# A software-pipelined Mamba-2 group loop on one core: state matmuls moved ahead of the transposes, out-projection three slots behind its pair

## The reference

```python
h = x * rsqrt(mean(x*x) + EPS) * norm_w             # x: 2 x 256 tokens, 512 wide
proj = einsum('bsd,od->bso', h, in_proj_w)           # gate 8192, hBC 8192 + 2048, dt 128
hBC = silu(causal_conv(hBC, conv_w, conv_b))         # 4 taps
hid, B, C = split(hBC)                               # 128 heads of 64; 8 groups of 128 for B and C
dt = softplus(dt + dt_bias); A_full = -exp(A_log) * dt
hid_dt = hid * dt
M = (C_i . B_j) * exp(segsum(A_full))                # per head, i >= j
y = M @ hid_dt + Dp * hid
yg = y * silu(gate)
yg = yg * rsqrt(mean over the group's 1024 channels of yg**2 + EPS) * gnorm_w
x = residual + yg @ out_proj_w.T
```

## Time and profile before

| | us |
|---|---|
| median of 3 runs (range) | 827.75 (827.05 to 828.55) |
| profiled execution | 823.68 |
| its span | 821.9 |
| TensorE busy | 790.5 (96%), 4319 matmuls |
| VectorE busy | 612.4 (75%) |
| ScalarE busy | 603.8 (73%) |
| GpSimd busy | 615.7 (75%) |
| groups 1 to 6 | 92.1 each, from loop to loop |

### The profile page before, as it was taken

The page is one execution under the profiler, slowest core; times in us unless marked ns, Lnnn a source line. Parts: engine busy times, 40 slices in busy tenths (PEclk is TensorE's granted clock), DMA queues, the critical chain, the costliest instruction groups (busy, mean ns, idle before and its releaser), DMA issues.

```text
span 821.9 us, 13293 instructions
## 1 busy us (share of the span) xinstructions
PE 790.5 (96%) x4319; PEld 610.7 (74%) x4322; DVE 612.4 (75%) x752; ACT 603.8 (73%) x1052; POOL 615.7 (75%) x552
## 2 busy tenths in 40 slices
PE   8799899999999999999999999999999999989897
PEld 7567677777777777777777777777777777767664
DVE  6768987777786867776786867776786867787774
ACT  5778786888688876878688886878688886877442
POOL 6669966799578986799578986799578985795231
PEclk9999999999999999999999999999999999999999
DMA  8433324334234324333233314334233324340001
GB/s 332 148 92 127 129 65 155 128 120 138 90 128 128 128 64 154 128 128 128 90 128 128 128 64 154 128 128 128 90 128 128 128 65 155 128 154 1 4 2 52
DMA packets 48812, 94.93 MB, mean 116 GB/s; under 512 B 3952, under 2 KB 36848, under 8 KB 48784
## 3 DMA queue, kind: packets, MB, share of 16 engines
q1 hardware_dynamic: 48496, 94.06, 34.6%
q10 hardware_dynamic: 288, 0.52, 0.2%
HBM read 93.26 MB, written 1.31 MB: 115 GB/s over the span
## 4 chain that ended last, share of the span: by engine, by line
PE 62%; DVE 17%; ACT 11%; issue 7%; DMA 0%; POOL 0%; ACTq 0%; DVEq 0%
PE ps_z L1093 19%; PE ps_out L1196 15%; PE ps_h L1093 13%; PE ps_y L1183 7%; DVE conv_bc L728 4%; DVE conv L728 4%; ACT decay L531 4%; PE ps_t L1066 2%; ACT L531 2%; ACT conv L477 2%; DVE v L846 2%; DVE yg L852 2%; DVE decay L786 2%; ACT conv_bc L461 1%; DVE y_lo L858 1%
## 5 line engine op out<-in xcount | busy, mean ns | idle before, releaser
L728 DVE SCALAR_TENSOR_TENSOR conv<-ps_h,w_raw,conv 128x510 f32<-128x510 f32 (+2 forms) x192 | 143.2, 746 | 102.1 <-ACT conv L477 97.6
L531 ACT ACTIVATE decay<-csx,cs_own 128x256 f32<-128x256 f32 (+1 forms) x512 | 184.4, 443 | 1.0
L297 POOL TENSOR_TENSOR win_lo<-w_raw,win_hi 128x1024 fp32r<-128x1024 f32 x64 | 153.1, 2392 | 0.9 <-DMA csx<-cs_rows 0.9
L399 POOL TENSOR_TENSOR sqacc<-sqacc,sq 128x512 f32<-128x512 f32 x47 | 69.8, 1486 | 107.1 <-ACT sq L567 107.1
L786 DVE TENSOR_TENSOR decay<-decay,cbm 128x1536 f32<-128x1536 f32 x64 | 126.0, 1969 | 3.6 <-ACT decay L531 3.6
L1183 PE MATMUL ps_y<-decay,hid_dt 128*64 128x256 f32 (+1 forms) x1024 | 98.9, 336 | 16.1 <-DVE hid_dt L835 16.1
L539 ACT ACTIVATE hidT<-conv 128x512 f32<-128x512 f32 x64 | 40.5, 633 | 100.5 <-DVE conv L728 100.5
L1183 PEld LDWEIGHTS ps_y<-decay,hid_dt 128*64 128x64 f32 x1024 | 64.1, 138 | 58.9 <-DVE hid_dt L835 21.8
L337 POOL TENSOR_SCALAR_AFFINE_SELECT csx<-csx 128x512 f32<-128x512 f32 x128 | 102.1, 823 | 0.5 <-DMA csx<-cs_rows 0.5
L1196 PE MATMUL ps_out<-wout_hi,y_lo 128*128 128x512 f32 x252 | 99.9, 396 | 0.0
L1196 PE MATMUL ps_out<-wout_hi,y_hi 128*128 128x512 f32 x252 | 99.5, 395 | 0.0
(11 more groups left out here) (314 smaller groups left out, 1514.2 us busy)
## 6 DMA issues: line engine op xcount, KB each, us to landing
w_raw<-in_wmain SPq DMA_DIRECT2D x64, 772.0 KB, 4.3
csx<-cs_rows SPq DMA_DIRECT2D x128, 256.0 KB, 3.5
bc_raw<-in_wbc SPq DMA_DIRECT2D x8, 517.0 KB, 3.5
ctx_raw<-in_ctx SPq DMA_DIRECT2D x1, 2048.0 KB, 16.2
bc_raw<-in_wffn SPq DMA_DIRECT2D x2, 512.0 KB, 3.8
out_x<-acc SPq DMA_DIRECT2D x4, 256.0 KB, 2.1
acc<-in_x ACTq DMA_DIRECT2D x2, 256.0 KB, 3.9
acc<-in_x SPq DMA_DIRECT2D x2, 256.0 KB, 3.7
```

Of the source, the lines that this page charges most:

```text
L297: eng.tensor_tensor(win_lo[:, r2, :], w_raw[:, r4, 0:W_IN], win_hi[:, r2, :].bitcast(f32), ALU.subtract).then_inc(low_win, 1)
L399: eng.tensor_tensor(sqacc[:], sqacc[:], sq[:, (k - 1) % 2, :], ALU.add).then_inc(pool_sq, 1)
L531: done = eng.activation(decay[:, r2, b, h, lo:lo + n], csx[:, r2, b, h, lo:lo + n], ACT.Exp, bias=cs_own[:, r2, t, h:h + 1])
L728: eng.scalar_tensor_tensor(out=out_b[:, :, back:], in0=src_b[:, :, 0:S - back], scalar=w[:, TAPS - 1 - back:TAPS - back], in1=out_b[:, :, ...
```

## The change

Each part by engine:

- TensorE: a slot is now hidden projection of s, gate projection of s, out-projection of s-3, state matmuls of s-1, transposes of s. At k = 0 and k = 7, where the gate's bank `ps_z` still holds a B or C projection, the out-projection stands ahead of the gate projection. The C.B products move behind the gate projection and use `ps_h` in place of `ps_z`; the channel sums move to k = 2.
- VectorE: `combine` of s-2 comes first, then `hid_dt` of s-1, the group's add (now k = 3), the mask of s-1, the conv of s, `y_lo` of s-2.
- ScalarE: the decays of s come first in slot s (before: the decays of s+1 came last), then the tap, then `y_hi` and `sq` of s-2, the SiLU of B or C, `hidT`, `gate`.
- GpSimd: the sum of squares (of s-3) goes ahead of the splits, the split of the out-weights is that of pair s (before: s+1) and stands behind the selects, `rstd` is raised at the head of k = 3.
- SP: the same transfers. `y_lo` of a pair is now made two slots behind it (before: one), so the wait for it ends one slot later; a wait for `wout_lo` of the same pair is added.

The core of the diff (line numbers of the two files differ by up to 24):

```diff
 
                     if late(s - 3):
                         eng.wait_ge(dve_ylo, s - 3)
+                        eng.wait_ge(low_wout, s - 3)
                     eng.dma_start(w_raw[:, r, :], wmain_d[s]).then_inc(w_in[r], 16)
...
+                if k == 3 and not first:
+                    eng.wait_ge(dve_ms, g)
+                    eng.tensor_tensor(rstd[:], ms[:], half_neg[:], ALU.pow).then_inc(pool_rstd, 1)
                 if not (last and k == PPG - 1):
                     eng.wait_ge(w_in[n4], 16 * (2 * g + (k + 1) // 4 + 1))
-                    if first and 0 < k < 3:
+                    if late(s):
                         eng.wait_ge(pe_gate, s)
-                    if late(s - 2):
-                        eng.wait_ge(pe_out, s - 2)
+                if late(s - 3):
+                    eng.wait_ge(pe_out, s - 3)
...
+                sum_squares(s, g, k, first)
                 if not (last and k == PPG - 1):
                     split_in(n4, (k + 1) % 2)
-                    split_out(n4)
                     eng.wait_ge(csx_in[1 - r2], 32 * (4 * g + (k + 1) // 2 + 1))
                     lower_in(n4, (k + 1) % 2, s + 2)
                     select(1 - r2)
-                    lower_out(n4, s + 2)
+                split_out(r4)
+                lower_out(r4, s + 1)
                 if k == 4:
                     eng.tensor_scalar(wbc_hi[:], bc_raw[:, 0:BC_W], 1.0, 0.0, ALU.mult, ALU.add).then_inc(hi_wbc, 1)
                     lower_bc(g + 2)
 
-                sum_squares(s, g, k, first)
-                if k == 1 and not first:
-                    eng.wait_ge(dve_ms, g)
-                    eng.tensor_tensor(rstd[:], ms[:], half_neg[:], ALU.pow).then_inc(pool_rstd, 1)
...
-                if k == 1 or (first and k == 0):
+                n = (k - 3) % PPG
+                gs = g if k >= 3 else g - 1
+                if n == 0 or (first and k < 3):
                     return
-                eng.wait_ge(act_sq, s)
-                if k == 2:
-                    if late(g):
-                        eng.wait_ge(pe_ss, g)
+                eng.wait_ge(act_sq, s - 2)
+                if n == 1:
+                    if late(gs):
+                        eng.wait_ge(pe_ss, gs)
                     eng.tensor_tensor(sqacc[:], sq[:, 0, :], sq[:, 1, :], ALU.add).then_inc(pool_sq, 1)
                 else:
...
+                if first and k == 1:
+                    tap(s, g, k)
+                    decays(s, k)
+                    scale_context(0)
+                    hidden(s, k)
+                    gates(s, k)
+                    return
+                decays(s, k)
+                if k == PPG - 1 and not last:
+                    tap_bc(0, g + 1, ps_z, conv_bc[:])
                 if k == 0:
                     tap_bc(1, g, ps_z, conv_bc[:])
-                    silu_bc(1, g, conv_bc[:])
-                if k == PPG - 1 and not last:
-                    tap_bc(0, g + 1, ps_z, conv_bc[:])
-                    silu_bc(0, g + 1, conv_bc[:])
-                if not (first and k == 1):
-                    tap(s, g, k)
-                hidden(s, k)
-                gates(s, k)
+                tap(s, g, k)
                 finish_y(s, g, k, first)
-                if not (last and k == PPG - 1):
-                    decays(s + 1, k + 1)
                 if first:
                     scale_context(k - 1)
                 if last and k == 4:
                     scale_context(PPG - 1)
+                if k == PPG - 1 and not last:
+                    silu_bc(0, g + 1, conv_bc[:])
+                if k == 0:
+                    silu_bc(1, g, conv_bc[:])
+                hidden(s, k)
+                gates(s, k)
...
+                if not (first and k < 2):
+                    combine(s, k)
                 if not (first and k == 0):
                     scale_hidden(s, k)
-                if k == 2 and not first:
+                if k == 3 and not first:
                     add_group(g - 1)
+                if not (first and k == 0):
+                    mask(s, g, k)
                 if k == PPG - 1 and not last:
                     conv_group(0, g + 1, ps_z, conv_bc[:])
-                if k == 0:
-                    conv_group(1, g, *((ps_y, gate[:, 1, :]) if first else (ps_z, conv_bc[:])))
-                if first and k == 0:
-                    conv_hidden(s, k)
+                if k == 0 and not first:
+                    conv_group(1, g, ps_z, conv_bc[:])
+                conv_hidden(s, k)
+                if not (first and k < 2):
+                    lower_y(s, k)
+                if k == 0 and first:
+                    conv_group(1, g, ps_y, gate[:, 1, :])
...
                     eng.tensor_copy(cbm[:, 0, :], ps_t[:, 0:MJ]).then_inc(dve_cb, 1)
-                if not (first and k == 0):
-                    conv_hidden(s, k)
-                if k == 1 and not first:
+                if k == 2 and not first:
                     mean_squares(g - 1)
-                if first and k == PPG - 1:
-                    eng.wait_ge(pre_pool, POOL_RSTD + TT)
-                if not (first and k == 0):
...
-                eng.wait_ge(act_exp, s + 1)
-                if k == 0:
-                    eng.wait_ge(dve_cb, 2 * g + 2)
-                eng.tensor_tensor(decay[:, r2], decay[:, r2], cbm[:].unsqueeze(2).broadcast_to([P, B, 2, MJ]),
-                                  ALU.mult).then_inc(dve_m, 1)
-                if not (first and k == 0):
-                    lower_y(s, k)
...
+            def mask(s, g, k):
+
+                eng.wait_ge(act_exp, s)
+                if k == 1:
+                    eng.wait_ge(dve_cb, 2 * g + 2)
+                q2 = (k - 1) % 2
+                eng.tensor_tensor(decay[:, q2], decay[:, q2], cbm[:].unsqueeze(2).broadcast_to([P, B, 2, MJ]),
+                                  ALU.mult).then_inc(dve_m, 1)
...
-                q2, q4 = (k - 1) % 2, (k - 1) % 4
-                eng.wait_ge(pe_y, s)
-                eng.wait_ge(act_hid, s)
-                if late(s - 1):
-                    eng.wait_ge(dve_yg, s - 1)
+                q2, q4 = k % 2, (k - 2) % 4
+                eng.wait_ge(pe_y, s - 1)
+                eng.wait_ge(act_hid, s - 1)
+                if late(s - 2):
+                    eng.wait_ge(dve_yg, s - 2)
...
-                eng.wait_ge(dve_convbc, 3)
-                project(ps_z[:], win_hi[:, 0, KT * P:], win_lo[:, 0, KT * P:], pe_gate)
-
             def slot(eng, s, g, k, first, last):
                 r2 = k % 2
+
+                turned = k == 0 or k == PPG - 1 and not last
 
                 eng.wait_ge(low_win, s + 1)
                 if late(3 * s):
                     eng.wait_ge(dve_conv, 3 * s)
+                if k == 1:
+                    eng.wait_ge(dve_cb, 2 * g + 1)
                 project(ps_h[:], win_hi[:, r2, 0:KT * P], win_lo[:, r2, 0:KT * P], pe_hid)
                 if first and k == 0:
                     start_up()
+                if turned and not (first and k == 0):
+                    project_out(s, g, k)
+
+                if late(s):
+                    eng.wait_ge(act_gate, s)
+                if k == 0:
+                    eng.wait_ge(dve_convbc, 3 if first else 6 * g + 6)
+                if k == PPG - 1 and not last:
+                    eng.wait_ge(dve_convbc, 6 * (g + 1) + 3)
+                project(ps_z[:], win_hi[:, r2, KT * P:], win_lo[:, r2, KT * P:], pe_gate)
+                if not turned and not (first and k < 3):
+                    project_out(s, g, k)
+                if k == 0:
+                    products_of_bc(s, g)
+                if k == 2 and not first:
+                    sum_channels(s, g - 1)
                 if not (first and k == 0):
                     scan_heads(s, k)
-                if k == 0:
-
-                    eng.wait_ge(act_bc, 2 * g + 2)
-                    if late(s):
-                        eng.wait_ge(act_gate, s)
-                    for b, bank in ((1, ps_y if first else ps_z), (0, ps_t)):
-                        q = b * S
-                        mm(bank[:, 0:S], bcT[:, 0, q:q + P], bcT[:, 1, q:q + S], start=True, stop=True)
-                        mm(bank[:, S:MJ], bcT[:, 0, q + P:q + S], bcT[:, 1, q + P:q + S], start=True,
-                           stop=True).then_inc(pe_cb, 1)
-                if k == 1 and not first:
-                    sum_channels(g - 1)
-
-                if not (first and k == 0):
-                    eng.wait_ge(act_gate, s)
-                    if k == 0:
-                        eng.wait_ge(dve_cb, 2 * g + 1)
-                    if k == PPG - 1 and not last:
-                        eng.wait_ge(dve_convbc, 6 * (g + 1) + 3)
-                    project(ps_z[:], win_hi[:, r2, KT * P:], win_lo[:, r2, KT * P:], pe_gate)
-                if not (first and k < 2):
-                    project_out(s, g, k)
 
                 eng.wait_ge(act_hid, s + 1)
                 if k == 0:
```

(13 more changed lines are left out.)

61 lines of the change are left out of this document (35 added, 26 removed).

## The result

| | before | after |
|---|---|---|
| median us (range), 4 runs each | 827.4 (822.68 to 828.55) | 855.7 (854.04 to 858.85) |
| ratio to before | | 1.0358, 95% interval 1.0307 to 1.0408 |
| profiled execution, its span | 823.68, 821.9 | 855.27, 853.5 |
| a middle group | 92.1 | 97.1 to 97.9 |

The changed kernel is slower by 28 us. The forecast was 849 us in a range of 809 to 862; with the slower side at 0.71, its sign, its place and its mechanism held. Its size was 7 us short in the medians.

A forecast was written before the change was run, and what follows sets the result against it. TensorE, busy 96% of the span, was taken as the bound. Terms -3.2, -21.7, +5.1, +27, +6.8 and +7.2 gave +21 us on 823.7, so 845; the median's 4.1 made 849 us, range 809 to 862.

The forecast's parts named there:

- the slower side: Whole kernel: the chance given to the changed kernel being slower than before, 0.71.
- (a): Seams between TensorE's matmul blocks, ps_z behind the state matmuls: 0.05 us saved in each of 64 slots, -3.2 us.
- (b): TensorE's waits for hid_dt and bcT, and the clock they lowered, all go: -21.7 us.
- (c): First group: new TensorE waits for hidT and cb products, as ScalarE forms decays inside the slot: +5.1 us.
- (d): Late w_raw load delays GpSimd's weights, so TensorE waits: +27 us in six groups, +6.8 first, +7.2 last.
- rival 3: Each wait at slot 6 lowers the clock, engines collide every pass, no seam gained: +41, 869 us; chance 0.08.
- late hidT at slot 6: End of slot 6: late selects delay ScalarE's decays and hidT, so the transposes wait 1.0 us more a group.
- (d), k = 3: Slot k=3, group's adds ahead of the mask: conv and hidT late for the transposes, 0.45 us waited a group.
- Rival 1: Weights arrive in time, win_lo ready before 20.7 in every group: 809 us; chance 0.20.
- likeliest case: The forecast itself, with 2.8 to 5.9 us lost a group: 838 to 858 us; chance 0.60.
- Rival 2: Lower end of (d), 2.4 us a group, paid by the old waits: -0.6, 827 us; chance 0.12.

The follow-up runs named there:

- e1: Changed kernel, but ScalarE copies the D and norm columns aside and SP's w_raw load waits for conv, not y_lo: 806.4 us, ratio 0.9757.
- e6: e1 with SP's wait set back to y_lo as in the changed kernel, the small tile kept: 857.82 us, ratio 1.0408.
- e7: Changed kernel with 14 idle matmuls on TensorE at the head of k=6, ahead of its wait for win_lo: 843.47 us, ratio 1.0237.
- e9: Changed kernel with three quarters of VectorE's mask left out in slot k=5 of each group: 837.97 us, ratio 1.0161.
- e5: Kernel before, old order, with the edit of e1 alone (small tile and early w_raw load): 834.93 us, ratio 1.0119.

## Why the prediction was right, and where its sizes were off

| term, us | forecast | measured | from |
|---|---|---|---|
| (a) seams, 64 slots | -3.2 | about -2.2, and 0.5 a group more | 10.45 to 10.42 a regular slot; k = 0 to 2 from 33.9 to 33.2 |
| (b) old waits and their clock | -21.7 | gone | 0.7 us left in e1 |
| (c) new waits, first group | +5.1 | +3.5, and 1.5 of clock | 2.03 for bcT (1.15 before), 2.03 and 0.60 for hidT |
| (d) six middle groups | +27 | +37.9 | 97.36 against 91.05 in e1, x 6 |
| (d) first, last group | +6.8, +7.2 | +5.5, +7.9 | slots k=3 to 6 against 10.42 and 13.27 |
| all on the span | +21 | +31.6 | 821.9 to 853.5 |

The last row also has the 1.5 us ahead of the first slot; some 1.6 us of it stay unplaced. Against e1's mean middle group (91.29; two of the six take 91.73) the six middle groups lose 36.4 and not 37.9.

**The mechanism (d) held link by link.** y_lo of k=3 ends, w_raw is issued behind it, GpSimd idles for it, and the wait appears once a group at the slot it was put at. Forecast from the end of the transposes at slot 4's head: w_raw lands at 3.8 to 4.6, win_lo for slot 5 ends at 8.6 to 10.1, that for slot 6 at 23.4 to 24.5. Measured from 356.5: 5.3, 10.5 and 24.7, each later than the forecast's upper end: y_lo ends 11.5 us behind the start of its slot in place of 10.3 to 11.1, and this load takes 4.9 us from its issue to cs_own in place of 4.3. TensorE is later as well, done with its transposes at 21.3 in place of 20.7, as slots 4 and 5 take 10.65 each. So the wait, 3.39 to 3.57 us in the six middle groups, fell into the forecast's 2.7 to 3.8 (3.1 taken) in part because two errors cancel. The slots price the whole of (d) at 51.3 us and e6 against e1 at 50 to 54, where 41 was forecast. Of its other signs, the idle time of GpSimd ahead of cs_own was forecast at 1 to 4 us and is 5.61 here and 6.6 at most.

**(d), the clock.** The step that was mis-sized most. The sum had nothing for it and gave it to rival 3 with 0.08, on the ground that a 3.36 us wait hadn't lowered the clock in the earlier trace rows. k=6 was long behind the wait in every middle group and e7 shows 1.4 to 1.6 us for each, 8.9 in the six. One row where it stayed up was no rule: in e9 waits of 1.89 and 1.90 us are followed by slots of 14.8 and of 13.26.

**(d), late hidT at slot 6: +1.0 a group, measured nothing in the middle groups.** e7 has that slot at full clock without a wait there; in its first group it waits 1.30 and in its last 0.58. The step took 5.1 us from the decays to the conv from a stretch that includes ScalarE's table load of 1.28, but the load had been done during the wait for the selects: from 383.88 to the conv at 387.46 are 3.6 us. ScalarE, then VectorE, after:

```profile
377.34 1.28 ACT L538 ACT_TABLE_LOAD   x1 [1.47 <-PE ps_y L1204]
383.88 2.88 ACT L538 ACTIVATE decay<-csx,cs_own 128x256 f32<-128x256 f32 x8 [5.26 <-POOL csx L336]
...
387.46 2.31 DVE L736 SCALAR_TENSOR_TENSOR conv<-ps_h,w_raw,conv 128x510 f32<-128x510 f32 x3 [4.70 <-ACT conv L480]
```

**(d), k = 3: 0.45 forecast, 1.0 measured** (slots of 11.18 to 12.05 against 10.42). e1 brings it to nothing in most groups, so the adds ahead of the mask are not its cause as the forecast had it; they are only late when GpSimd is: rstd comes 0.31 us late and the mask, behind win_lo, takes 2.95. The sum had nothing for k = 4 either, which loses 0.2 a group in the mean.

**(a), (b), (c).** Of the seam of 0.09 a part comes back, as the transposes now take 0.42 to the next matmul (442.10 to 442.52) where they took 0.36 (350.87 to 351.23 before). In (c) the waits are 1.6 us less than forecast, but the clock, for which (c) had nothing, falls behind one of them: TensorE waits 2.03 us for hidT in the first group, and the next stretches take 1.7 us each to the one behind in place of 0.93 (the granted clock is 0.68 from 45 to 50).

```profile
43.45 0.66 PE L1080 MATMUL ps_t<-ident,hidT 128*128 128x128 f32 x4 [2.03 <-ACT hidT L546]
...
44.89 1.91 PE L1107 MATMUL ps_h<-hT_lo,win_hi 128*128 128x512 f32 x4
46.59 1.85 PE L1107 MATMUL ps_h<-hT_hi,win_lo 128*128 128x512 f32 x4
```

e1, which has all of the change but (d), is 16.3 us under before by the spans (821.9 to 805.6) and 20.4 by the medians; (a), (b) and (c) as forecast give -19.8.

**The rivals.** Rival 1 (weights in time, 809) is what e1 built: 806.4. It didn't come true by itself. Rival 3 was nearer than its 0.08 says: the clock fell at every wait at slot 6, and a middle group lost 6.3 us, where rival 3 had 6.7 and the forecast's likeliest case 2.8 to 5.9. What kept the time under its 869 was the rest: seams were gained, and the two outer groups lost 13.4 and not 18. Rival 2 asked for an rstd slipped in early; GpSimd raised it behind wout_lo, as forecast.

**Where luck came in.** That 855.7 lies inside the likeliest case (838 to 858) is partly luck. The forecast added 4.1 us, by which the profiled execution of before was under the median; that of after is only 0.4 under its own. By the forecast's own way from span to median +31.6 would give 859. And the hidT that never came late in the middle groups (6 us too much) paid for a part of the clock (8.9 us too little).

## What to carry to other kernels

When a step is moved to a later slot, look up what its completion frees, and follow that count into the transfer queue: here the last reader of a 772 KB buffer wanted one column of it (and v another), and copying the two aside (0.19 us on ScalarE) turned 3.6% slower into 2.4% faster. Price a lateness at every consumer up to where the backlog is gone, and as an edge and not as a slope. A wait of TensorE of some 2 us may cost a second time in the clock behind it: 1.5 us in three of six middle groups of e9, nothing in the others.

## What had not been expected of the hardware

- Which of VectorE and GpSimd goes first moved 1.3 us a group in the old order (e5), where the starts of yg and wbc_hi lie within 0.14 us of each other: the same mask takes 1.75, 2.59 or 3.95 us by what GpSimd has begun.
- TensorE ran at 0.50 of its clock for some 3 us behind an idle time of 3.45 us, while filler matmuls of 3.46 us in the same place kept it at 1.00 (e7).
- Behind idle times of about 2 us the next slot was 1.5 us longer in three cases of six (e9), by the same amount as behind 3.45 us. In the first group of the changed kernel the clock stayed at 1.00 behind a wait of 2.03 us (31.44) and fell behind the next one of 2.03 (43.45); in e1 it was the other way about (2.05 us at 30.72, where it fell, and 2.14 at 45.65, where it didn't). What decides that is left open by these runs.
